# A GRU with a mixture of experts behind it: the experts' first product as one matmul of 256 columns for the weights' high parts and one of 128 for the low parts

## What is computed

```
def cell(h, x):
    gi = x @ W_ih + b_ih
    gh = h @ W_hh + b_hh
    r = sigmoid(i_r + h_r);  z = sigmoid(i_z + h_z)
    n = tanh(i_n + r * h_n)
    return (1 - z) * n + z * h
...
combine = the top 2 of softmax(x / norm @ router_w), made to sum to 1
for e in range(8):
    out = out + combine[:, e, None] * (x @ Wa[e] @ Wb[e])
return input + out
```

## Time and profile before

| | us |
|---|---|
| median of 3 runs | 1042.76 (1042.55 to 1043.12) |
| the profiled execution | 1042.57 |
| its span | 1040.8 |
| TensorE busy | 1011.4 (97%) |
| VectorE busy | 860.0 (83%) |
| ScalarE busy | 722.6 (69%) |
| GpSimd busy | 299.0 (29%) |

### The profile page before, as it was taken

The page is one execution under the profiler, slowest core; times in us unless marked ns, Lnnn a source line. Parts: engine busy times, 40 slices in busy tenths (PEclk is TensorE's granted clock), DMA queues, the critical chain, the costliest instruction groups (busy, mean ns, idle before and its releaser), DMA issues.

```text
span 1040.8 us, 67010 instructions
## 1 busy us (share of the span) xinstructions
PE 1011.4 (97%) x28409; PEld 828.4 (80%) x28409; DVE 860.0 (83%) x3215; ACT 722.6 (69%) x2824; POOL 299.0 (29%) x762
## 2 busy tenths in 40 slices
PE   5789999999999999999999999999999999999997
PEld 3677888888888888888888888888888888888875
DVE  6889888888888888888888888888888888888886
ACT  7687666767666767667767667667766767766663
POOL 2032232322233332233332233332233332223223
PEclk9999999999999999999999999999999999999999
DMA  8230111111111111111111111111111011110001
GB/s 295 84 94 17 30 32 29 30 27 30 29 32 29 29 27 30 29 32 30 29 28 28 29 32 32 27 30 27 29 32 32 26 30 28 29 32 20 9 9 33
DMA packets 49522, 39.24 MB, mean 38 GB/s; under 512 B 34676, under 2 KB 39112, under 8 KB 49224
## 3 DMA queue, kind: packets, MB, share of 16 engines
q1 hardware_dynamic: 48376, 31.41, 11.1%
q10 hardware_dynamic: 848, 3.54, 1.0%
HBM read 18.94 MB, written 8.39 MB: 26 GB/s over the span
## 4 chain that ended last, share of the span: by engine, by line
PE 91%; DVE 5%; ACT 2%; DMA 1%; issue 1%; POOL 0%; ACTq 0%; DVEq 0%; POOLq 0%
PE ybank L1014 18%; PE pairs L883 17%; PE obank L1037 15%; PE gates L958 11%; PE gates L963 10%; PE nbank L912 7%; PE zbank L973 5%; PE zbank L969 5%; DVE tr L762 1%; PE nbank L994 1%; DMA wih<-in_L_cond_W_ih 1%; DVE pre L765 1%; DVE acc L815 1%; ACT nn L624 1%; DVE pre L771 1%
## 5 line engine op out<-in xcount | busy, mean ns | idle before, releaser
L883 PEld LDWEIGHTS pairs<-wx,xs 128*32 128x32 f16 x6144 | 140.7, 96 | 105.8 <-issue 101.7
L883 PE MATMUL pairs<-wx,xs 128*32 128x256 f16 x6144 | 215.6, 275 | 0.0
L1014 PE MATMUL ybank<-hparts,wa 128*128 128x128 f16 x3024 | 212.5, 220 | 0.0
L458 POOL TENSOR_TENSOR y<-y 128x128 f16<-128x128 f32 x256 | 111.7, 436 | 348.1 <-ACT y L658 190.0
L1037 PE MATMUL obank<-wb,y 128*128 128x512 f16 x738 | 199.3, 379 | 0.0
L1014 PEld LDWEIGHTS ybank<-hparts,wa 128*128 128x128 f16 x3024 | 169.8, 98 | 26.9
L762 DVE STREAM_TRANSPOSE tr<-gates 128x256 f32<-128x256 f32 x256 | 115.1, 450 | 72.4 <-PE gates L963 68.5
L616 ACT ACTIVATE rr<-pre 128x64 f32<-128x64 f32 x256 | 65.7, 257 | 155.6 <-DVE pre L765 155.2
L958 PE MATMUL gates<-whh,st 128*32 128x256 f16 x4080 | 155.8, 273 | 11.3 <-DVE st L788 10.8
L963 PE MATMUL gates<-whh,hparts 128*32 128x256 f16 x4080 | 155.9, 273 | 0.0
L815 DVE SCALAR_TENSOR_TENSOR acc<-obank,comb,acc 128x512 f32<-128x512 f32 x184 | 136.9, 744 | 0.2
(11 more groups left out here) (134 smaller groups left out, 1701.4 us busy)
## 6 DMA issues: line engine op xcount, KB each, us to landing
out<-outb SPq DMA_DIRECT2D x63, 128.0 KB
xin<-in_x SPq DMA_DIRECT2D x58, 128.0 KB
wih<-in_L_cond_W_ih ACTq DMA_DIRECT2D x4, 768.0 KB, 7.7
whh<-in_L_cond_W_hh SPq DMA_DIRECT2D x4, 768.0 KB, 11.8
wih<-in_L_ffn_Wb SPq DMA_DIRECT2D x8, 256.0 KB, 2.7
xs<-xh SPq DMA_TRANSPOSE x116, 2.8
wih<-in_L_ffn_Wa SPq DMA_DIRECT2D x4, 256.0 KB, 4.2
whh<-in_L_ffn_Wa SPq DMA_DIRECT2D x4, 256.0 KB, 2.6
```

Source lines behind the costliest of these rows:

```text
L458: nc.gpsimd.tensor_tensor(y[:, m % YB, 1, :], y32[:, :], y[:, m % YB, 0, :], ALU.subtract).then_inc(ylo_ready, 1)
L883: mm = nc.tensor.matmul(bank[32 * j:32 * j + 32, P:3 * P], turned(b, k, ph)[:, t0:t0 + 2 * B], wx[:, pw, k, j, :], start=False, stop=(k == ...
L1014: mm = nc.tensor.matmul(y_at(m)[:, 0:P], wa[:, pw, k, e, :], hparts[:, f % HB, k, :, ph * B:(ph + 1) * B], start=(n == 0), stop=(n == 3 * ...
```

## The change

`expert_down` issues two matmuls for each of the four slices: one of the weights' high part with all 256 columns of the block's `hparts` (high and low parts of the states), and one of the weights' low part with the 128 high columns, accumulated onto the high columns' places. Of each 32 columns in PSUM the first 16 then hold the sum of two terms and the last 16 the product of the states' low part. `y32` takes all 256 columns. The high part of `y` is the rounding of the first 16 of each 32. `low_y` takes the difference as before, into a new tile `y_rest` in float32, and a second GpSimd operation adds the other 16 columns to it and writes the low part. There is a new semaphore between the two, and the first operation also waits until the last pair is done.

```diff
             def low_y(m):
...
+                wait(pool, ylo_ready, m)
+                nc.gpsimd.tensor_tensor(y_rest[:, :].rearrange("p (s b) -> p s b", b=B), y32[:, :, 0:B],
+                                        y[:, m % YB, 0, :].rearrange("p (s b) -> p s b", b=B), ALU.subtract
+                                        ).then_inc(rest_ready, 1)
+                pool.wait_ge(rest_ready, m + 1)
+                nc.gpsimd.tensor_tensor(y[:, m % YB, 1, :].rearrange("p (s b) -> p s b", b=B),
+                                        y_rest[:, :].rearrange("p (s b) -> p s b", b=B), y32[:, :, B:2 * B], ALU.add
                                         ).then_inc(ylo_ready, 1)
...
             def split_y(m):
...
-                nc.scalar.activation(y32[:, :], y_at(m)[:, 0:P], ACT.Copy, scale=1 / PART_SCALE).then_inc(y32_ready, 1)
+                nc.scalar.activation(y32[:, :, :], y_at(m), ACT.Copy, scale=1 / PART_SCALE).then_inc(y32_ready, 1)
...
             def expert_down(m):
...
                 for k in range(K):
-                    for ph, pw in TERMS:
-                        mm = nc.tensor.matmul(y_at(m)[:, 0:P], wa[:, pw, k, e, :],
-                                              hparts[:, f % HB, k, :, ph * B:(ph + 1) * B],
-                                              start=(n == 0), stop=(n == 3 * K - 1))
-                        n += 1
+                    nc.tensor.matmul(y_at(m), wa[:, 0, k, e, :], hparts[:, f % HB, k, :, :], start=(k == 0), stop=False,
+                                     skip_group_check=True)
+                    mm = nc.tensor.matmul(y_at(m)[:, :, 0:B], wa[:, 1, k, e, :], hparts[:, f % HB, k, :, 0:B],
+                                          start=False, stop=(k == K - 1), skip_group_check=True)
                 mm.then_inc(y_done, 1)
```

More of the change, by code:

```diff
@@ L137, in gru_moe_kernel @@
         comb = sb("comb", [P, NE])
-        y32 = sb("y32", [P, P])
+        y32 = sb("y32", [P, S, 2 * B])
+        y_rest = sb("y_rest", [P, P])
         y = sb("y", [P, YB, 2, P], F16)
@@ L164, in y_at @@
         def y_at(m):
-            return ybank if m < LAST else last_y[(m - LAST) % 2]
+            return (ybank if m < LAST else last_y[(m - LAST) % 2])[:, 0:2 * P].rearrange(
+                "p (s b) -> p s b", b=2 * B)
         def o_at(m):
@@ L228, in gru_moe_kernel @@
         y32_ready = sem("y32_ready")
+        rest_ready = sem("rest_ready")
         ylo_ready = sem("ylo_ready")
@@ L457, in low_y @@
                 wait(pool, o_done, m - YB + 1)
-                nc.gpsimd.tensor_tensor(y[:, m % YB, 1, :], y32[:, :], y[:, m % YB, 0, :], ALU.subtract
+                wait(pool, ylo_ready, m)
[5 more added lines that the diff above has]
+                                        y_rest[:, :].rearrange("p (s b) -> p s b", b=B), y32[:, :, B:2 * B], ALU.add
                                         ).then_inc(ylo_ready, 1)
@@ L657, in split_y @@
                 wait(act, o_done, m - YB + 1)
-                nc.scalar.activation(y[:, m % YB, 0, :], y_at(m)[:, 0:P], ACT.Copy, scale=1 / PART_SCALE
-                                     ).then_inc(yhi_ready, 1)
+                nc.scalar.activation(y[:, m % YB, 0, :].rearrange("p (s b) -> p s b", b=B), y_at(m)[:, :, 0:B], ACT.Copy,
+                                     scale=1 / PART_SCALE).then_inc(yhi_ready, 1)
                 wait(act, ylo_ready, m)
-                nc.scalar.activation(y32[:, :], y_at(m)[:, 0:P], ACT.Copy, scale=1 / PART_SCALE).then_inc(y32_ready, 1)
+                nc.scalar.activation(y32[:, :, :], y_at(m), ACT.Copy, scale=1 / PART_SCALE).then_inc(y32_ready, 1)
             def beside(n):
@@ L1010, in expert_down @@
                     pe.wait_ge(weights_split, splits_before(wa_split_at[m]))
-                n = 0
                 for k in range(K):
-                    for ph, pw in TERMS:
-                        mm = nc.tensor.matmul(y_at(m)[:, 0:P], wa[:, pw, k, e, :],
-                                              hparts[:, f % HB, k, :, ph * B:(ph + 1) * B],
-                                              start=(n == 0), stop=(n == 3 * K - 1))
-                        n += 1
+                    nc.tensor.matmul(y_at(m), wa[:, 0, k, e, :], hparts[:, f % HB, k, :, :], start=(k == 0), stop=False,
+                                     skip_group_check=True)
+                    mm = nc.tensor.matmul(y_at(m)[:, :, 0:B], wa[:, 1, k, e, :], hparts[:, f % HB, k, :, 0:B],
+                                          start=False, stop=(k == K - 1), skip_group_check=True)
                 mm.then_inc(y_done, 1)
```

## The result

The changed kernel takes 1060.36 us (median of 6 runs, 1059.88 to 1061.14) where the kernel before takes 1042.76 (6 runs, 1042.55 to 1043.12): a ratio of 1.017, interval 1.0157 to 1.0183. It is 17.6 us slower. The forecast was 1066.5, with a range of 1050 to 1083. The profiled execution took 1061.14, its span is 1059.3. The sign, GpSimd's part in it and most of the terms came out as forecast; the two largest terms of a block were too large, because one rule in the working was wrong, and with it the place where the second GpSimd operation starts.

A forecast was written before the change was run, and what follows sets the result against it. TensorE was taken to bound the kernel, with the recurrence only 0.14 us of slack behind it. Later blocks 18.1, first blocks 1.5 and tail 4.3 made +23.9 on 1042.6: 1066.5 us, range 1050 to 1083.

The forecast's parts named there:

- What bounds the kernel: TensorE holds 91% of the span; behind it the recurrence through gates and new state has 0.14 us slack per step.
- TensorE's part: In `expert_down`, 8 matmuls in place of 12 keep 1536 columns, so each step saves only 0.01 us.
- Rival 3: A TensorE matmul costs by count, not columns: up to 0.14 us off per step, 1015 in all; chance 0.04.
- ScalarE's part: L662 reads 256 columns of PSUM in place of 128, nearest row 0.385 us: +0.11 per step, hidden by idle time.
- GpSimd's pair: L458 becomes two dependent operations, 0.40 and 0.49 us with 0.08 between: 0.97 together, 0.54 more than before.
- Rivals 1 and 2: 1: pair 0.88 us or less, 1050, chance 0.15 with Rival 4; 2: short runs cost 0.05 per operation, 1080, 0.18.
- Rival 4: GpSimd does not hold L765 when its inputs are strided, or holds it shorter: 1050; chance 0.15 together with rival 1.
- First and second `split_x` step: The pair, starting behind `split_x`, ends late and delays L765: +0.08 us in the first, +0.02 in the second.
- Squares step: Step from 500.96: GpSimd starts 0.14 us later and L765 ends at 503.16 in place of 502.84: +0.18.
- Router's step: Step from 504.81: L451 behind the pair ends late, so `route`'s first matmul L988 starts late: +0.40 us.
- First blocks: The blocks before the steady pattern, where `st` binds anyway: an estimate of +1.5 us.
- Tail: After the last step ScalarE and GpSimd alternate on one `y32`, 1.52 us per expert, so GpSimd binds: +4.3 us.

The follow-up runs named there:

- e1: Changed kernel with a single GpSimd operation on the 128 high columns, the states' low parts' product left out: 1040.94 us, ratio 0.9979 to the kernel before.
- e2: Kernel before, 12 matmuls and 128 columns kept, with two dependent GpSimd operations, the second adding zeros: 1061.44 us, ratio 1.0174.
- e6: Changed kernel with squares first, a GpSimd memset between the pair's operations in three steps of a block, and two `y32`: 1046.92 us, ratio 1.0032.
- e7: Changed kernel with only a GpSimd memset between the pair's operations in both `split_x` steps and the squares step: 1058.66 us, ratio 1.0143.
- e3: Changed kernel with the second operation of the squares' split moved ahead of the GpSimd pair: 1050.64 us, ratio 1.007 to the kernel before.
- e9: e6 with the memset in the second `split_x` step widened to 256 columns: 1044.47 us, ratio 1.0015 to the kernel before.
- e8: New form only for experts 12 to 247, old form elsewhere; squares first, one `y32`, memsets as in e9: 1042.18 us, ratio 0.9991 to the kernel before.

## Why the prediction came out as it did

- **What bounds the kernel.** Right. The 0.14 us of slack is what the first `split_x` step shows: L776 is 0.23 late, the step grows by 0.10.
- **TensorE's part.** Right: 0.01 forecast, 0.010 measured in e1. Rival 3, by count, is out. The Trainium skill's page "TensorE: Matmul & The Clock Gate", section "Back-to-back issue gap", has 81 ns for each matmul of 128 columns in a stream with weight loads. The traces do not agree: 57 ns before, and 0.67 us for the eight now.
- **ScalarE's part.** Right: 0.377 for 0.385, hidden.
- **GpSimd's pair.** Right in sum, 0.96 for 0.97. Short runs of 16 cost it nothing: the first operation takes 0.43, as L458 did, and e2's pair without such runs leads to the same steps. Rivals 1 and 2 are out. Rival 4 is out as it stands, for GpSimd does hold L776 (0.52 at 443.44), but its outcome for the squares step came true for another reason, the order of the starts.
- **First and second `split_x` step.** Right: +0.10 and +0.03 for +0.08 and +0.02. There the second operation starts 0.09 and 0.15 ahead of L776, so the rule used and the true one agree.
- **Squares step: the step that failed.** "L765 ends at the later of its start + 0.29 and the GpSimd end + 0.15" was read from rows in which GpSimd had started first. It leaves out who was first. By it the squares step should have grown by 0.18; it grew by 0.00, since in 26 of the 28 blocks L468 and L776 start within 4 ns of each other and VectorE wins. Over 28 blocks that is 5.0 us too much, where the whole forecast was 6.1 too high.
- **A second slip in the same step, and luck.** The right rule alone would not have given 0.00. The prediction has the first operation start 1.08 into this step, which is what it does (446.87 less 445.79), and gives it 0.40: with the gap of 0.08 the second one then starts at 1.56, 0.03 ahead of L765 at 1.59, and holds it. (In step 201 of the changed kernel, a first `split_x` step, it does start 0.03 ahead, and L776 takes 0.57.) Only because the first operation takes 0.43, as L458 did, do the two start together. So the 0.00 hangs on a few ns; had the pair come 0.01 earlier, the step would have cost about what was forecast, as the second `split_x` step of e6 and e7 shows with its 4.01.
- **Router's step.** Right in its cause (e3), too large: +0.32 for +0.40. The 0.14 carried over from the squares step was not there, since that step was no longer bound by `st`: L464 starts 1.18 into the step (450.81 less 449.63), forecast 1.31. A part of it comes back because VectorE now holds GpSimd: L468 takes 0.50 for 0.46 behind L776, and L455 takes 0.47 for 0.40 behind L782, which starts 0.02 ahead of it. Over 31 blocks the term was 2.5 us too large.
- **First blocks.** The estimate was 1.5, and steps 8 to 19 grew by 1.8; the other 1.0 of this profile is the clock in step 1. The growth is in steps 11 (0.36) and 17 to 19 (about 0.3 each), with 0.1 or less in most others. Steps 17 to 19 are explained by e3, e7 and e9. What part the splitting of the weights on VectorE has in the rest was not tried.
- **Tail.** Right: the turn is 1.51 as computed and binds for the last four experts. The last `expert_up` starts 20.9 us behind the last step's first matmul (1054.16 less 1033.31), before 16.7: +4.1 for +4.3. What follows it, the last sums and the stores, was 0.6 shorter in this profile, so that the whole tail is +3.5.
- **What would show it.** "Waits of L958 for `st` in some 90 steps" did not show: under that name the list has 17. The weight load of L969 has more, 49 waits put down to "issue" where L958 had 24, and all 26 of them in steps 24 to 247 stand at the end of the first `split_x` step. So the waits show one step of a block that `st` bounds, where three were forecast.

## What to carry to other kernels

A GpSimd operation beside a VectorE operation with two SBUF inputs holds it if it starts first, and is held itself if it does not, so before adding one, compare their starts, not only their ends: starting 0.10 us behind was free here, and starting 0.09 us ahead made the VectorE operation of the critical loop 0.23 us longer. Where the starts come out within some 0.01 us of each other, take the term as either of two values and not as one. An operation added to an idle engine is not free when something on that engine's row feeds the critical engine: here 10 of 17.6 us went because one small sum stood behind the added operation, and moving it ahead gave them back. Where work on TensorE is bound by columns, merging matmuls saves about 2.5 ns for each matmul that goes, so what is added elsewhere to make it possible must cost less than that.

## What the runs showed of the hardware

- The order of a VectorE and a GpSimd operation is settled within some ns: with GpSimd 6 ns ahead VectorE's 0.29 us became 0.596, at 5 ns ahead it stayed 0.29 and GpSimd's 0.46 became 0.61 (steps of e7). The kernels whose starts lie that close have two lengths of the same step, 3.84 and 4.01 us, and their time hangs on it (e7, e6).
- Held, a VectorE operation of 128 columns ends 0.15 us behind GpSimd's end (443.96 against 443.81). Held, GpSimd's operation of 128 columns ends about 0.31 behind VectorE's end (451.82 against 451.51). Each is less than the operation's own length, 0.29 and 0.46.
- A GpSimd memset did not hold the former L765. The case that can tell is rare, since in most steps the memset ends too soon after VectorE's start. One late step of e9, first GpSimd's line and then VectorE's:

```profile
1000.37 0.20 POOL L470 MEMSET idle<- 128x128 f32 x1
1000.38 0.29 DVE L778 TENSOR_TENSOR pre<-tr 128x128 f32<-128x128 f32 x1
```

  The memset starts first and ends 0.19 behind VectorE's start. With a hold, L778 would end 0.15 behind that and take 0.34; it takes 0.29. The same step of e7 and e8 has it too.
- A matmul whose PSUM output lies in runs of 16 columns out of 32 takes no longer than one into 128 columns in a row (e1: the four pairs take no more than the 12 did, and the step is 0.010 shorter).
